# Two pairs of heads at a time: scores and value products of a causal softmax attention in double turns on one Trainium2 core

## The chip, the cores and the metric

The kernel runs on one core of a Trainium2 chip (trn2). The metric is the device time in microseconds (us) of one execution, the median of several. Five engines work from their own instruction streams and meet at semaphores: TensorE (PE; its weight loads are shown apart as PEld), VectorE (DVE), ScalarE (ACT), GpSimd (POOL) and SyncE (SP), which here only issues DMAs.

## What is computed

The input x is (32, 256, 128), float32. Six residual blocks follow each other. The first four (two small feed-forward products with tanh, a linear attention, a spectral product) work on groups of four 128-row tiles; this change leaves them alone. The last two are the causal softmax attention with 16 heads, and a spectral product on its result:

```python
q = jnp.einsum('qdh,bcd->bhcq', Q, x) * sq
k = jnp.einsum('qdh,bcd->bhcq', K, x) * sq
v = jnp.einsum('vdh,bcd->bhcv', V, x) * sv
att = jnp.einsum('bhcq,bhCq->bhcC', q, k) / d_query
att = jnp.where(causal, att, -jnp.inf)
p = jax.nn.softmax(att, axis=-1)
y = jnp.einsum('bhcC,bhCv->bhcv', p, v)
z = jnp.einsum('dvh,bhcv->bcd', W, y) * (math.sqrt(d_embed / d_value) / num_heads)
...
x = x + _L1_attn_ref(_layernorm(x, axis=-1), L1_attn_Q, L1_attn_K, L1_attn_V, L1_attn_W)
x = x + 0.5 * _L1_ffn_ref(_layernorm(x, axis=-1), L1_ffn_w_freq_real, L1_ffn_w_freq_imag, L1_ffn_bias)
```

## The kernel before, in words

Everything stays in SBUF. After the first four blocks (about 265 us) comes the softmax stage: 32 batches of 256 tokens, each worked through in 8 turns, one turn per pair of heads. Pair number n = 8b + p is pair p of batch b; j = p % 2 names the buffer. The order of the work is written out by hand in one `batch` function per engine, and each engine runs its own list; `batches` unrolls the first two and last two batches and loops over the rest, two at a time.

A pair passes through these steps:

- QK, `qk_product` (L1013 to L1015): queries and keys of the two heads, six matmuls over all 128 rows, into the one bank BANK_QK. ACT copies the bank as rounded values (`qk_high`, L739), DVE writes what the rounding left (`qk_low`, L501). Only then is the bank free for the next QK.
- S, `scores` (L1028): twelve matmuls that each use half of the rows of the array (64), the two heads side by side, into two of the four S banks.
- mask and row maximum on DVE (`mask_scores`, L515), exp with row sums on ACT (`exp_head`, L753, once per head), 1/sum on DVE (`inv_sum`, L523), the scaling on POOL (`scale_probs`, L321 and L323).
- T, `probs_transpose` (L1041): six transposes over all 128 rows, four into BANK_T and two into the bank behind it. DVE copies the four (`probs_T`, L530), ACT the two (L762).
- PV, `products` (L1058): eight matmul passes that each use half of the columns of the array, into the other half of that second bank. ACT copies y out (`y_out`, L777).

Before the change, turn n of PE is: QK of pair n+3, S of n+2, PV of n-1, one extra piece, T of n. The extra pieces, E below, are: in turn 0 the transposes XT (L1005) and ZT (L1075), in turns 1 to 3 the output projection Z of the batch before (`project_out`, L1067, in steps of 12, 12 and 8 of its 32 matmul passes, the last with the spectral product SP, L1080 and L1083), in turns 4 to 7 V, the values of the next batch (`values`, L1047 to L1049). The end of the stage (the last pairs, the last projection and spectral product) is written out behind the loops.

The steps of the loop that matter, in PE's list:

```python
pe.wait_ge(qklo_ready, count(n + 3))
qk_product(n + 3, (p + 3) % PAIRS, jb if p + 3 < PAIRS else 1 - jb, 1 - j)
```

## Time and profile before

| | |
|---|---|
| three timed runs | 1364.82, 1366.13, 1367.47 us; median 1366.13 us |
| the profiled execution | 1366.64 us, of which the span is 1364.9 us |
| busy over the span | PE 1303.4 us (95%), PEld 1081.4 (79%), DVE 1030.2 (75%), ACT 970.6 (71%), POOL 592.0 (43%) |
| mean granted clock of TensorE | 0.991 of full speed |

The profile comes from one execution; its times are from the span's start. "Busy" counts instructions that do work. A matmul's record is longer than the distance to the next one's start, since matmuls are pipelined, so PE can show as busy without a gap and still lose time between two starts; distances of starts tell more than busy shares.

### The profile page before, as it was taken

How to read it: one execution, taken by the hardware profiler on the slowest of the kernel's cores; microseconds unless marked ns; L12 is line 12 of the kernel's file. 1: busy time of each engine (PE TensorE's matmuls, PEld its weight loads, DVE VectorE, ACT ScalarE, POOL GpSimd, SP SyncE). 2: the span in 40 equal slices, each digit the busy share in tenths (PEclk: the TensorE clock that was granted, in tenths of full speed). 3: DMA queues.
4: the chain of work that ended last, by engine and by line, in shares of the span. 5: the costliest groups of instructions: out<-in, count | busy, mean ns of one | idle time of the engine just before them, and what ended most of it. 6: DMA issues, size and time to landing. Idle time of an engine off the chain costs nothing.

```text
span 1364.9 us, 38712 instructions
## 1 busy us (share of the span) xinstructions
PE 1303.4 (95%) x11331; PEld 1081.4 (79%) x11331; DVE 1030.2 (75%) x4813; ACT 970.6 (71%) x3377; POOL 592.0 (43%) x913
## 2 busy tenths in 40 slices
PE   5799977899999999999999999999999999999996
PEld 4688866778888888888888888888888888888884
DVE  6977689777777777777777777777777777777763
ACT  4754467587777777777777777777777777777772
POOL 5821158344444444444444444444444444444442
PEclk9999999999999999999999999999999999999997
DMA  8000000000000000000000000000000000000000
GB/s 206 1 1 0 1 1 1 0 2 2 2 9 0 8 0 8 0 8 0 8 0 8 0 8 0 8 0 8 0 8 0 8 0 8 0 8 0 9 2 16
DMA packets 14301, 11.79 MB, mean 9 GB/s; under 512 B 710, under 2 KB 12523, under 8 KB 14059
## 3 DMA queue, kind: packets, MB, share of 16 engines
q1 hardware_dynamic: 14240, 11.19, 3.0%
q8 instruction: 23, 0.38, 0.1%
q14 instruction: 28, 0.22, 0.1%
q10 hardware_dynamic: 10, 0.00, 0.0%
HBM read 7.00 MB, written 4.19 MB: 8 GB/s over the span
## 4 chain that ended last, share of the span: by engine, by line
PE 90%; issue 3%; DVE 3%; ACT 2%; DMA 1%; POOL 1%; SPq 1%; DVEq 0%; POOLq 0%; ACTq 0%
PE ps L1028 16%; PE ps L1058 15%; PE ps L1041 13%; PE ps L1067 10%; PE ps L1013 5%; PE ps L1014 4%; PE ps L1015 4%; PE ps L1047 4%; PE ps L1048 2%; PE ps L1049 2%; PE ps L900 2%; PE ps L922 2%; PE ps L942 2%; PE ps L960 1%; PE ps L1083 1%
## 5 line engine op out<-in xcount | busy, mean ns | idle before, releaser
L321 POOL TENSOR_TENSOR pr<-pr,rinv 128x256 f32<-128x256 f32 x256 | 158.1, 618 | 611.6 <-DVE rinv L523 611.6
L753 ACT ACTIVATE pr<-ps,neg_max 128x128 f32<-128x128 f32 (+1 forms) x1024 | 418.5, 428 | 0.0
L515 DVE CUSTOM_DVE_ANT_0 ps<-ps,mask 128x128 f32<-128x128 f32 (+1 forms) x1024 | 334.7, 386 | 0.0
L530 DVE COPY pT<-ps 128x512 f32<-128x512 f32 x256 | 177.2, 692 | 194.3 <-PE ps L1041 194.0
L323 POOL TENSOR_TENSOR pr<-pr,rinv 128x512 f32<-128x512 f32 x256 | 266.4, 1040 | 0.0
L501 DVE TENSOR_TENSOR qk_lo<-ps,qk_hi 128x512 fp32r<-128x512 f32 x256 | 176.2, 688 | 71.7 <-ACT qk_hi L739 71.7
L1058 PE MATMUL ps<-pT,space 128*64 128x256 f32 (+1 forms) x2048 | 224.3, 340 | 2.3 <-DVE pT L530 2.3
L739 ACT CAST qk_hi<-ps 128x512 fp32r<-128x512 f32 x256 | 150.4, 587 | 106.9 <-PE ps L1015 106.7
L1041 PE MATMUL ps<-ident,pr 128*128 128x128 f32 x1536 | 217.2, 274 | 4.7 <-POOL pr L323 3.3
L753 ACT ACTIVATION_READ_ACCUMULATOR pr<-ps,neg_max 128x1 f32 x1024 | 217.8, 213 | 0.0
L1041 PEld LDWEIGHTS ps<-ident,pr 128*128 128x128 f32 x1536 | 179.0, 141 | 31.2 <-issue 8.4
L762 ACT COPY pT<-ps 128x256 f32<-128x256 f32 x256 | 95.4, 373 | 145.0 <-PE ps L1041 133.2
L1058 PEld LDWEIGHTS ps<-pT,space 128*64 128x64 f32 x2048 | 124.7, 136 | 75.5 <-DVE pT L530 3.4
L1028 PE MATMUL ps<-qk_hi 64*128 64x128 f32 (+1 forms) x1024 | 169.1, 327 | 0.0
L1013 PE MATMUL ps<-x_hi,wqk_hi 128*128 128x256 f32 x512 | 166.1, 324 | 0.1
L1014 PE MATMUL ps<-x_lo,wqk_hi 128*128 128x256 f32 x512 | 143.8, 281 | 0.0
L1015 PE MATMUL ps<-x_hi,wqk_lo 128*128 128x256 f32 x512 | 143.6, 281 | 0.0
L515 DVE DVE_READ_ACCUMULATOR2_ANT neg_max<- 128x1 f32 x1024 | 142.8, 139 | 0.0
L1028 PE MATMUL ps<-qk_lo,qk_hi 64*128 64x128 f32 (+1 forms) x1024 | 142.6, 275 | 0.0
L1067 PE MATMUL ps<-wz,space 128*128 128x128 f32 x1024 | 141.9, 288 | 0.5 <-ACT z_xT L783 0.5
L1028 PE MATMUL ps<-qk_hi,qk_lo 64*128 64x128 f32 (+1 forms) x1024 | 142.2, 274 | 0.0
L1067 PEld LDWEIGHTS ps<-wz,space 128*128 128x128 f32 x1024 | 124.0, 195 | 16.8 <-issue 15.9
(165 smaller groups left out, 2374.5 us busy)
## 6 DMA issues: line engine op xcount, KB each, us to landing
out<-x_all SPq DMA_DIRECT2D x16, 256.0 KB, 2.3
x_all<-L_attn_x SPq DMA_DIRECT2D x1, 768.0 KB, 6.7
x_all<-L_attn_x SPq DMA_DIRECT2D x1, 512.0 KB, 4.6
space<-L_attn_Q SPq DMA_DIRECT2D x1, 512.0 KB, 15.6
space<-L_attn_K SPq DMA_DIRECT2D x1, 512.0 KB, 9.7
space<-L_attn_V SPq DMA_DIRECT2D x1, 512.0 KB, 11.3
space<-L_attn_W SPq DMA_DIRECT2D x1, 512.0 KB, 11.7
dft_s<-dft SPq DMA_DIRECT2D x1, 192.0 KB, 2.5
```

The source lines that it names most:

```text
L323: nc.gpsimd.tensor_tensor(pr[:, j, :, 1:3, :].rearrange("p h b k -> p h (b k)"), pr[:, j, :, 1:3, :].rearrange("p h b k -> p h (b k)"), r[ ...
L501: nc.vector.tensor_tensor(qk_lo[:, j].rearrange("p s k -> p (s k)"), ps[:, BANK_QK, :], qk_hi[:, j].rearrange("p s k -> p (s k)").bitcast( ...
L515: last = nc.vector.tensor_tensor_reduce(o, o, mask[:, T - w:T], -1.0, -MASKED, ALU.add, ALU.min, neg_max[:, j, 2 * h + qt:2 * h + qt + 1])
L530: nc.vector.tensor_copy(pT[:, j].rearrange("p h b q -> p (h b q)")[:, 0:512], ps[:, BANK_T, :]).then_inc(pTa_ready, 1)
L753: last = nc.scalar.activation(dst, ps[:, BANK_S + 2 * j + h, qt * P:qt * P + w], ACT.Exp, bias=neg_max[:, j, at:at + 1], scale=-1.0, accum ...
L1013: mm(o, wqk_hi[:, s, of_pair], x_hi[:, jb, :], start=True, stop=False, skip_group_check=True)
L1014: mm(o, wqk_hi[:, s, of_pair], x_lo[:, jb, :], start=False, stop=False, skip_group_check=True)
L1015: last = mm(o, wqk_lo[:, s, of_pair], x_hi[:, jb, :], start=False, stop=True, skip_group_check=True)
L1028: last = mm(ps[:, BANK_S + 2 * j + h, qt * P:qt * P + w], q[of_head, j, 0, qt * P:(qt + 1) * P], key[of_head, j, 1, 0:w], start=(k == 0), ...
L1041: last = tr(ps[:, BANK_T + k // 4, (k % 4) * P:(k % 4 + 1) * P], pr[:, j, k // 3, k % 3, :], ident[:])
L1058: last = mm(y_bank[k * DV:(k + 1) * DV, kt * P:T], vv[:, jb, kt, h * DV:(h + 1) * DV], pT[:, j, k, 0:2, :] if kt == 0 else pT[:, j, k, 2, ...
L1067: last = mm(ps[:, BANK_X, t * D:(t + 1) * D], yT[:, j, p, t * P:(t + 1) * P], wz[:, p, :], start=(p == 0), stop=(p == PAIRS - 1), skip_gro ...
```

## The change

Turns are paired. In each turn p, PE now does QK of pair n+2, the extra piece, and T of pair n-1. In an odd turn there follow S of n+1, S of n+2, PV of n-2 and PV of n-1, in a row. The extra pieces move by one turn: V of the next batch in turns 5 to 7 and the following 0, XT and ZT in turn 1, Z in turns 2 to 4.

`pr` gets a third buffer. The last two transposed blocks of a pair and its y share a half of bank 7 (BANK_Y) one after the other: T of an even pair writes the first half, T of an odd pair the second; PV of n-2 writes its y over the first half and PV of n-1 over the second, once the blocks have been copied out. `y_out` is called once per two turns and copies both halves as one 128x512 block (for the first pair of every second batch, where the ring of y wraps, two of 128x256).

ACT and DVE follow: an even turn of ACT begins with exp of the first head of pair n+1, then the QK copy of n+2, and ends with exp of the second head; an odd turn does both heads of the next even pair and then `y_out`. DVE masks two pairs in a row at the end of an odd turn. The diff, cut to its core (what is left out renames arguments, keeps waits in step, and adapts the steps ahead of the loops):

```diff
-        pr = sb("pr", [P, 2, 2, 3, P])
+        pr = sb("pr", [P, 3, 2, 3, P])
...
+        BANK_QK, BANK_S, BANK_X, BANK_T, BANK_Y = 0, 1, 5, 6, 7
...
-        LN_TURN, W_TURN, ADD_TURN, V_TURN, Z_TURN = 1, 1, 4, 4, 5
+        X_TURN, LN_TURN, W_TURN, V_TURN, Z_TURN = 1, 2, 2, 5, 6
+
+        def pr_of(p):
+
+            return 0 if p % 2 == 0 else 1 + p % PAIRS // 2 % 2
...
-                    if not (first and p == 0):
-                        probs_T(n - 1, 1 - j)
-                    inv_sum(n, j)
-                    if p == LN_TURN and not last:
+                    if p % 2 == 0:
+                        inv_sum(n, j)
+                    if p == 0 and above_0(b - 1):
+                        z_norm(b - 2)
+                    if p == X_TURN + 1 and not last:
                         x_low(b + 1, 1 - jb)
                     if p == LN_TURN and has_batch(b + 2):
                         ln_soft_stats(b + 2, jb)
-                    if p == LN_TURN + 2 and has_batch(b + 2):
+                    if p == LN_TURN + 3 and has_batch(b + 2):
                         ln_soft_norm(b + 2, jb)
-                    if p == ADD_TURN and not first:
+                    if p == Z_TURN and not first:
+                        z_stats(b - 1)
+                    if p % 2 == 1:
+                        inv_sum(n, j)
+                    if not (last and p >= PAIRS - 2):
+                        qk_low(n + 2, j)
+                    if p == W_TURN + 2 and not first:
                         add_z(b - 1)
                         if above_0(b - 1):
                             add_spectral(b - 2, b)
-                    if p == Z_TURN and not first:
-                        z_stats(b - 1)
-                    if p == Z_TURN + 1 and not first:
-                        z_norm(b - 1)
-                    if not (last and p >= PAIRS - 3):
-                        qk_low(n + 3, 1 - j)
-                    if not (last and p >= PAIRS - 2):
-                        mask_scores(n + 2, j)
+                    if not (first and p == 0):
+                        probs_T(n - 1, 1 - j)
+                    if p % 2 == 1 and not (last and p == PAIRS - 1):
+                        mask_scores(n + 1, 0)
+                        mask_scores(n + 2, 1)

             batches(dve, batch)
+            z_norm(B - 2)
             probs_T(B * PAIRS - 1, 1)
-            add_z(B - 1)
             add_spectral(B - 2, B)
+            add_z(B - 1, B + 1)
             z_stats(B - 1)
             z_norm(B - 1)
-            add_spectral(B - 1, B + 1)
+            add_spectral(B - 1, B + 2)
...
-            def exp_head(n, j, h):
...
                 act.wait_ge(max_ready, count(2 * n + (1 + h)))
                 if h == 0:
-                    if above_0(n - 1):
-                        act.wait_ge(pt_done, count(n - 1))
+                    kept = n - 1 if buf == 0 else n - 3
+                    if above_0(kept):
+                        act.wait_ge(pt_done, count(kept))
                     if above_0(n - 1):
                         act.wait_ge(rinv_ready, count(n - 1))
...
-                nc.scalar.copy(pT[:, j].rearrange("p h b q -> p (h b q)")[:, 512:768], ps[:, BANK_T + 1, 0:256]).then_inc(pTb_ready, 1)
+                nc.scalar.copy(pT[:, j].rearrange("p h b q -> p (h b q)")[:, 512:768], ps[:, BANK_Y, j * T:(j + 1) * T]).then_inc(pTb_ready, 1)
...
-            def y_out(b, jb, p):
-                act.wait_ge(pv_done, count(b * PAIRS + (p + 1)))
-                if p == 0:
-                    if above_0(b - 1):
-                        act.wait_ge(w_done, count(b - 1))
-                nc.scalar.copy(yT[:, jb, p, :], y_bank).then_inc(y_ready, 1)
...
+            def y_out(b, jb, p, first=False):
+
+                act.wait_ge(pv_done, count(b * PAIRS + p))
+                if p == 1 and above_0(b - 1):
+                    act.wait_ge(w_done, count(b - 1))
+                at = jb * PAIRS + p - 1
+                if at > 0:
+                    nc.scalar.copy(y_ring[:, (at - 1) * T:(at + 1) * T], ps[:, BANK_Y, :]).then_inc(y_ready, 1)
+                else:
+                    if not first:
+                        nc.scalar.copy(yT[:, 1, PAIRS - 1, :], ps[:, BANK_Y, 0:T])
+                    nc.scalar.copy(yT[:, 0, 0, :], ps[:, BANK_Y, T:2 * T]).then_inc(y_ready, 1)
...
             def batch(b, jb, first=False, last=False):
                 for p in range(PAIRS):
                     n, j = b * PAIRS + p, p % 2
-                    if not (first and p == 0):
-                        probs_T(n - 1, 1 - j)
-                    if not (last and p >= PAIRS - 3):
-                        qk_high(n + 3, 1 - j)
-                    if not (last and p >= PAIRS - 1):
-                        exp_head(n + 1, 1 - j, 0)
-                        exp_head(n + 1, 1 - j, 1)
-                    if p > 0:
-                        y_out(b, jb, p - 1)
-                    elif not first:
-                        y_out(b - 1, 1 - jb, PAIRS - 1)
-                    if p == 0 and above_0(b - 1):
+                    if p % 2 == 0:
+                        exp_head(n + 1, 1, 0, pr_of(p + 1))
+                    if not (last and p >= PAIRS - 2):
+                        qk_high(n + 2, j)
+                    if p == X_TURN and above_0(b - 1):
                         z_xT_out(b - 2)
-                    if p == 0 and not last:
+                    if p == X_TURN and not last:
                         x_high(b + 1, 1 - jb)
                     if p >= V_TURN and not last:
                         values_out(b + 1, 1 - jb, p - V_TURN)
+                    if p == 0 and not first:
+                        values_out(b, jb, 3)
+                    if not (first and p == 0):
+                        probs_T(n - 1, 1 - j)
+                    if p % 2 == 0:
+                        exp_head(n + 1, 1, 1, pr_of(p + 1))
+                    else:
+                        if not (last and p == PAIRS - 1):
+                            exp_head(n + 1, 0, 0, 0)
+                            exp_head(n + 1, 0, 1, 0)
+                        y_out(b, jb, p, first)
...
             batches(act, batch)
+            z_xT_out(B - 2)
             probs_T(B * PAIRS - 1, 1)
-            y_out(B - 1, 1, PAIRS - 1)
-            z_xT_out(B - 2)
-            z_xT_out(B - 1)
+            last_y_out()
+            z_xT_out(B - 1, B + 1)
...
-            def probs_transpose(n, j):
+            def probs_transpose(n, j, buf, y_calls):
                 pe.wait_ge(pn_ready, count(n + 1))
                 if above_0(n):
                     pe.wait_ge(pTa_ready, count(n))
                 for k in range(6):
                     if k == 4 and above_0(n):
                         pe.wait_ge(pTb_ready, count(n))
-                        pe.wait_ge(y_ready, count(n))
-                    last = tr(ps[:, BANK_T + k // 4, (k % 4) * P:(k % 4 + 1) * P], pr[:, j, k // 3, k % 3, :], ident[:])
+                        pe.wait_ge(y_ready, count(y_calls))
+                    to = ps[:, BANK_T, k * P:(k + 1) * P] if k < 4 else ps[:, BANK_Y, j * T + (k - 4) * P:j * T + (k - 3) * P]
+                    last = tr(to, pr[:, buf, k // 3, k % 3, :], ident[:])
                 last.then_inc(pt_done, 1)
...
-            def products(n, p, jb, j):
+            def products(n, p, jb, j, half):
...
                 for kt in range(BT):
                     for k in range(2):
                         h = 2 * p + k
-                        last = mm(y_bank[k * DV:(k + 1) * DV, kt * P:T], vv[:, jb, kt, h * DV:(h + 1) * DV],
+                        last = mm(ps[k * DV:(k + 1) * DV, BANK_Y, half * T + kt * P:(half + 1) * T], vv[:, jb, kt, h * DV:(h + 1) * DV],
...
                 for p in range(PAIRS):
                     n, j = b * PAIRS + p, p % 2
-                    if not (last and p >= PAIRS - 3):
-                        pe.wait_ge(qklo_ready, count(n + 3))
-                        qk_product(n + 3, (p + 3) % PAIRS, jb if p + 3 < PAIRS else 1 - jb, 1 - j)
                     if not (last and p >= PAIRS - 2):
-                        scores(n + 2, jb if p + 2 < PAIRS else 1 - jb, j)
-                    if p > 0:
-                        products(n - 1, p - 1, jb, 1 - j)
-                    elif not first:
-                        products(n - 1, PAIRS - 1, 1 - jb, 1 - j)
-
-                    if p == 0:
+                        pe.wait_ge(qklo_ready, count(n + 2))
+                        qk_product(n + 2, (p + 2) % PAIRS, jb if p + 2 < PAIRS else 1 - jb, j)
+
+                    if p == 0 and not first:
+                        pe.wait_ge(v_ready, count(4 * b + 3))
+                        values(b, jb, 3)
+                    if p == X_TURN:
                         pe.wait_ge(v_ready, count(4 * (b + 1)))
                         if not last:
                             x_transpose(b + 1, 1 - jb)
...
                     if p >= V_TURN and not last:
                         values(b + 1, 1 - jb, p - V_TURN)
-                    probs_transpose(n, j)
+
+                    if not (first and p == 0):
+                        probs_transpose(n - 1, 1 - j, pr_of(p - 1), b * (PAIRS // 2) + p // 2)
+                    if p % 2 == 1:
+                        if not (last and p == PAIRS - 1):
+                            scores(n + 1, jb if p + 1 < PAIRS else 1 - jb, 0)
+                            scores(n + 2, jb if p + 2 < PAIRS else 1 - jb, 1)
+                        pe.wait_ge(pTb_ready, count(n))
+                        if p > 1:
+                            products(n - 2, p - 2, jb, 1, 0)
+                        elif not first:
+                            products(n - 2, PAIRS - 1, 1 - jb, 1, 0)
+                        products(n - 1, p - 1, jb, 0, 1)

             batches(pe, batch)
-            products(B * PAIRS - 1, PAIRS - 1, 1, 1)
             pe.wait_ge(out_ready, B - 2)
             spectral_transpose(B - 2)
+            probs_transpose(B * PAIRS - 1, 1, pr_of(PAIRS - 1), B * PAIRS // 2)
             pe.wait_ge(z_xT_ready, B - 1)
-            project_out(B - 1, 1, (0, BT * PAIRS))
             spectral_product(B - 2)
+            products(B * PAIRS - 1, PAIRS - 1, 1, 1, 0)
             pe.wait_ge(out_ready, B - 1)
+            project_out(B - 1, 1, (0, BT * PAIRS), only=True)
             spectral_transpose(B - 1)
             pe.wait_ge(z_xT_ready, B)
             spectral_product(B - 1)
```

PE in turn 5 of a looped batch, before, from the end of S through PV to V (each instruction waits for what stands in brackets):

```order
L1028 MATMUL ps<-qk_lo,qk_hi 128x256 x2
L1028 MATMUL ps<-qk_hi,qk_lo 128x256 x2
L1058 MATMUL ps<-pT,space 64x256 [waits pTb_ready,pTa_ready]
L1058 MATMUL ps<-pT,space 64x256
L1058 MATMUL ps<-pT,space 64x128 x2
L1147 REGISTER_ALU
L1047 MATMUL ps<-v_hi,x_hi 128x512 [waits v_ready]
```

The same place of an odd turn in the changed kernel, from the end of the second S to the next QK:

```order
L1050 MATMUL ps<-qk_lo,qk_hi 128x256 x2
L1050 MATMUL ps<-qk_hi,qk_lo 128x256 x2
L1081 MATMUL ps<-pT,space 64x256 [waits pTb_ready,pTa_ready]
L1081 MATMUL ps<-pT,space 64x256
L1081 MATMUL ps<-pT,space 64x128 x2
L1081 MATMUL ps<-pT,space 64x256 [waits pTb_ready,pTa_ready]
L1081 MATMUL ps<-pT,space 64x256
L1081 MATMUL ps<-pT,space 64x128 x2
L1035 MATMUL ps<-x_hi,wqk_hi 128x256 [waits qklo_ready]
```

The second PV has moved up to the first, and QK, which stood before S, now comes straight after PV.

ACT before, one turn (the QK copy, two heads of exp, y):

```order
L738 REGISTER_ALU [waits qk_done]
L739 CAST qk_hi<-ps 128x512 [waits s_done]
L743 REGISTER_ALU
L753 ACTIVATE pr,rsum<-ps,neg_max 128x128 [waits rinv_ready,pt_done,max_ready]
L753 ACTIVATE pr,rsum<-ps,neg_max 128x256
L753 ACTIVATE pr,rsum<-ps,neg_max 128x128 [waits max_ready]
L753 ACTIVATE pr,rsum<-ps,neg_max 128x256
L777 COPY space<-ps 128x256 [waits pv_done]
```

ACT in the changed kernel, from the exp of an odd turn into the even turn behind it:

```order
L762 ACTIVATE pr,rsum<-ps,neg_max 128x128 [waits rinv_ready,pt_done,max_ready]
L762 ACTIVATE pr,rsum<-ps,neg_max 128x256
L751 REGISTER_ALU
L762 ACTIVATE pr,rsum<-ps,neg_max 128x128 [waits max_ready]
L762 ACTIVATE pr,rsum<-ps,neg_max 128x256
L788 COPY space<-ps 128x512 [waits pv_done]
L751 REGISTER_ALU
L762 ACTIVATE pr,rsum<-ps,neg_max 128x128 [waits rinv_ready,pt_done,max_ready]
L762 ACTIVATE pr,rsum<-ps,neg_max 128x256
L744 REGISTER_ALU
L747 CAST qk_hi<-ps 128x512 [waits s_done,qk_done]
```

The QK copy now stands behind three heads of exp and the y copy.

## Rows read from the trace of the kernel before

**Rows 1.** Busy time by stretch: start:end, us, PE, PEld, DVE, ACT, POOL, PEclk, DMA

```profile
400.00:1300.00 900.00, 899.53 (x8266) 745.57 (x8264) 680.93 (x3247) 683.97 (x2510) 390.11 (x532) 1.00 0.01 4
...
1333.00:1364.90 31.90, 19.59 (x122) 14.48 (x118) 9.70 (x47) 8.14 (x33) 7.26 (x11) 0.74 0.06 17
```

**Rows 2.** Timeline, one turn with V: start, us from start to end, instruction

```profile
803.56 0.81 PE L1041 MATMUL ps<-ident,pr 128*128 128x128 f32 x6
804.13 0.37 PE L1013 MATMUL ps<-x_hi,wqk_hi 128*128 128x256 f32 x1
...
804.41 0.69 DVE L530 COPY pT<-ps 128x512 f32<-128x512 f32 x1 [0.50 <-PE ps L1041]
...
804.81 0.28 PE L1015 MATMUL ps<-x_hi,wqk_lo 128*128 128x256 f32 x1
805.02 0.33 PE L1028 MATMUL ps<-qk_hi 64*128 64x128 f32 x2
...
805.41 0.34 PE L1028 MATMUL ps<-qk_hi 64*128 64x256 f32 x2
805.58 0.28 PE L1028 MATMUL ps<-qk_lo,qk_hi 64*128 64x256 f32 x2
...
805.70 0.28 PE L1028 MATMUL ps<-qk_hi,qk_lo 64*128 64x256 f32 x2
805.91 0.87 PE L1058 MATMUL ps<-pT,space 128*64 128x256 f32 x8
806.71 0.50 PE L1047 MATMUL ps<-v_hi,x_hi 128*128 128x512 f32 x1
```

**Rows 3.** Timeline of PE at the stage's start: QK into V; QK after a wait

```profile
266.34 0.28 PE L1015 MATMUL ps<-x_hi,wqk_lo 128*128 128x256 f32 x1
266.46 0.39 PE L1047 MATMUL ps<-v_hi,x_hi 128*128 128x512 f32 x1
...
268.03 0.39 PE L1013 MATMUL ps<-x_hi,wqk_hi 128*128 128x256 f32 x1
...
268.73 0.28 PE L1015 MATMUL ps<-x_hi,wqk_lo 128*128 128x256 f32 x1
```

**Rows 4.** Timeline of PE near the end: T straight into S

```profile
1333.73 1.21 PE L1041 MATMUL ps<-ident,pr 128*128 128x128 f32 x6 [0.16 <-POOL pr L323]
1334.87 0.33 PE L1028 MATMUL ps<-qk_hi 64*128 64x128 f32 x2
```

**Rows 5.** Timeline of PE: Z of 12 and of 8 passes, SP, T

```profile
1319.61 1.60 PE L1067 MATMUL ps<-wz,space 128*128 128x128 f32 x12
...
1328.80 1.16 PE L1067 MATMUL ps<-wz,space 128*128 128x128 f32 x8
...
1330.35 0.82 PE L1041 MATMUL ps<-ident,pr 128*128 128x128 f32 x6
```

**Rows 6.** Line L1005 (XT, two per batch): its count, first and last start, from 400 us

```profile
L1005 PE MATMUL ps<-ident,xn x54: 272/300/330, 406.6 to 1282.5; 128*128 128x128 f32 x54
```

**Rows 7.** The same line from 270 to 310 us: the first looped XT and the next

```profile
L1005 PE MATMUL ps<-ident,xn x4: 272/301/330, 274.8 to 306.4; 128*128 128x128 f32 x4
```

**Rows 8.** Timeline of DVE: qk_low, mask of one head

```profile
805.82 0.69 DVE L501 TENSOR_TENSOR qk_lo<-ps,qk_hi 128x512 fp32r<-128x512 f32 x1 [0.64 <-ACT qk_hi L739]
806.44 0.30 DVE L515 CUSTOM_DVE_ANT_0 ps<-ps,mask 128x128 f32<-128x128 f32 x1
...
807.03 0.14 DVE L515 DVE_READ_ACCUMULATOR2_ANT neg_max<- 128x1 f32 x1
```

**Rows 9.** Timeline of ACT: the QK copy, two heads of exp, the next copy

```profile
805.20 0.59 ACT L739 CAST qk_hi<-ps 128x512 fp32r<-128x512 f32 x1 [0.42 <-PE ps L1015]
805.68 0.37 ACT L753 ACTIVATE pr<-ps,neg_max 128x128 f32<-128x128 f32 x1
...
807.28 0.39 ACT L777 COPY space<-ps 128x256 f32<-128x256 f32 x1
```

**Rows 10.** Timeline of PE at the end: the last projection

```profile
1349.56 6.46 PE L1067 MATMUL ps<-wz,space 128*128 128x128 f32 x32 [0.46 <-ACT z_xT L783]
```

More of the change, by code:

```diff
@@ L173, in build @@
         neg_max = sb("neg_max", [P, 2, 4]); rsum = sb("rsum", [P, 2, 4]); rinv = sb("rinv", [P, 2, 4])
-        pr = sb("pr", [P, 2, 2, 3, P])
+        pr = sb("pr", [P, 3, 2, 3, P])
         pT = sb("pT", [P, 2, 2, 3, P])
         vv = space[:, 0:2 * BT * H * DV].rearrange("p (r t n) -> p r t n", r=2, t=BT)
-        yT = space[:, 2 * BT * H * DV:].rearrange("p (r a t) -> p r a t", r=2, a=PAIRS)
+        y_ring = space[:, 2 * BT * H * DV:]
+        yT = y_ring.rearrange("p (r a t) -> p r a t", r=2, a=PAIRS)
         ps = ctx.enter_context(nc.psum_tensor("ps", [P, 8, 512], F32))
@@ L224, in build @@
         V_BANKS, W_BANKS = (4, 7), (0, 6)
[L225 to L227 removed]
+        BANK_QK, BANK_S, BANK_X, BANK_T, BANK_Y = 0, 1, 5, 6, 7
+        FIRST_V_BANKS = (BANK_X, BANK_T, BANK_Y, BANK_X)
         FFN1, LIN, FFN2, SPEC1 = range(4)
@@ L315, in _, with scale_probs @@
             phases(pool, [[(5, g_inv_std(phase))] for phase in (FFN1, LIN, FFN2, SPEC1)])
-            def scale_probs(n, j):
+            def scale_probs(n, j, buf):
                 pool.wait_ge(rinv_ready, count(n + 1))
                 r = rinv[:, j, :].rearrange("p (h q) -> p h q", h=2)
-                nc.gpsimd.tensor_tensor(pr[:, j, :, 0, :], pr[:, j, :, 0, :],
+                nc.gpsimd.tensor_tensor(pr[:, buf, :, 0, :], pr[:, buf, :, 0, :],
                                         r[:, :, 0:1].to_broadcast([P, 2, P]), ALU.mult)
-                nc.gpsimd.tensor_tensor(pr[:, j, :, 1:3, :].rearrange("p h b k -> p h (b k)"),
-                                        pr[:, j, :, 1:3, :].rearrange("p h b k -> p h (b k)"),
+                nc.gpsimd.tensor_tensor(pr[:, buf, :, 1:3, :].rearrange("p h b k -> p h (b k)"),
+                                        pr[:, buf, :, 1:3, :].rearrange("p h b k -> p h (b k)"),
                                         r[:, :, 1:2].to_broadcast([P, 2, 2 * P]), ALU.mult).then_inc(pn_ready, 1)
@@ L342, in batch @@
                 for p in range(PAIRS):
-                    scale_probs(b * PAIRS + p, p % 2)
+                    scale_probs(b * PAIRS + p, p % 2, pr_of(p))
                     if p == LN_TURN and has_batch(b + 2):
@@ L531, in probs_T, with add_z @@
                                       ps[:, BANK_T, :]).then_inc(pTa_ready, 1)
-            def add_z(b):
-                dve.wait_ge(w_done, count(b + 1))
+            def add_z(b, w_after=None):
+                dve.wait_ge(w_done, count(b + 1 if w_after is None else w_after))
                 nc.vector.tensor_tensor(xb(b), ps[:, BANK_X, 0:BT * D], xb(b), ALU.add).then_inc(x_ready, 1)
@@ L588, in _ @@
             mask_scores(0, 0)
-            qk_low(2, 0)
             mask_scores(1, 1)
@@ L770, in values_out, with last_y_out, z_xT_out @@
                 nc.scalar.copy(vv[:, j, c % 2, 512 * (c // 2):512 * (c // 2) + 512], ps[:, bank, :]).then_inc(v_ready, 1)
-            def y_out(b, jb, p):
-                act.wait_ge(pv_done, count(b * PAIRS + (p + 1)))
-                if p == 0:
-                    if above_0(b - 1):
-                        act.wait_ge(w_done, count(b - 1))
-                nc.scalar.copy(yT[:, jb, p, :], y_bank).then_inc(y_ready, 1)
-            def z_xT_out(b):
+            def y_out(b, jb, p, first=False):
[9 more added lines that the diff above has]
+                    nc.scalar.copy(yT[:, 0, 0, :], ps[:, BANK_Y, T:2 * T]).then_inc(y_ready, 1)
+            def last_y_out():
+                act.wait_ge(pv_done, B * PAIRS)
+                nc.scalar.copy(yT[:, 1, PAIRS - 1, :], ps[:, BANK_Y, 0:T]).then_inc(y_ready, 1)
+            def z_xT_out(b, w_after=None):
                 act.wait_ge(z_tr_done, count(b + 1))
                 if above_0(b):
-                    act.wait_ge(w_done, count(b + 1))
+                    act.wait_ge(w_done, count(b + 1 if w_after is None else w_after))
                 nc.scalar.copy(z_xT[:], ps[:, BANK_X, T:2 * T]).then_inc(z_xT_ready, 1)
@@ L793, in _ @@
             values_out(0, 0, 2, FIRST_V_BANKS[2])
-            qk_high(2, 0)
-            exp_head(0, 0, 0)
-            exp_head(0, 0, 1)
+            exp_head(0, 0, 0, 0)
+            exp_head(0, 0, 1, 0)
             values_out(0, 0, 3, FIRST_V_BANKS[3])
@@ L1061, in products, with project_out @@
                 last.then_inc(pv_done, 1)
-            def project_out(b, j, steps):
-                pe.wait_ge(y_ready, count(PAIRS * (b + 1)))
+            def project_out(b, j, steps, only=False):
+                pe.wait_ge(y_ready, count(PAIRS // 2 * (b + 1) + 1))
                 for k in range(*steps):
@@ L1068, in project_out @@
                               start=(p == 0), stop=(p == PAIRS - 1), skip_group_check=True)
-                if not above_0(b) and steps[1] == BT * PAIRS:
+                if (only or not above_0(b)) and steps[1] == BT * PAIRS:
                     last.then_inc(w_done, 1)
```

9 lines of the change are left out of this document (2 added, 7 removed).

## The prediction

> **What bounds the kernel now.** First the busy times by stretch [rows 1]: from 400 to 1300 us PE shows 899.5 of 900 us at full granted clock, DVE and ACT about 680 each. So the softmax stage is PE's, and only PE's distances from start to start say what a turn costs. Second, the length of a batch: the 54 starts of XT from 406.6 to 1282.5 are 27 batches, 26 distances, 33.69 us each [rows 6]. Third, one turn in the timeline [rows 2]. A piece that follows one of its own mode starts before the former ends by the pipelining: QK's first matmul starts 0.24 us before the end of T. A piece in another mode (all rows, half the rows, half the columns) starts only 0.07 us before that end: QK into S (805.09 against 805.02), S into PV, PV into V. Against the usual step of 0.12 that is 0.09 us lost at each of three changes per turn. V behind PV also opens slowly, 0.50 us for its first matmul, against 0.39 behind QK, where no change lies between [rows 3]: another 0.11.
>
> **What the change takes from PE.** From the same rows, in distances from a piece's start to the next one's start. Before: T 0.57, QK 0.89, S 0.89, PV 0.80 [rows 2], two turns 6.30; extra pieces per batch 4 V of 0.80, Z 1.44 twice, Z with SP 1.55, XT with ZT 0.49, together 8.1; sum 4 x 6.30 + 8.1 = 33.3, and 0.4 of small waits makes the 33.69.
>
> Now, for two turns: QK behind PV 0.70 + 0.12 = 0.82 (opening as after a wait [rows 3]), T 0.57, QK behind T 0.68 + 0.12 = 0.80, T into S 0.74 (six transposes last 0.81 [rows 2], and S starts 0.07 before T's end, 1334.87 against 1334.94 [rows 4]), S into S 0.80, S 0.89, PV into PV 0.71, PV 0.75. For the two joints that no row shows (S into S, PV into PV) I take the step within a mode; the upper end is that they cost the full 0.09. Sum 6.08. Extra pieces behind QK lose their opening: V 0.70, Z of twelve 12 x 0.11 = 1.34 (the difference of the 12 and the 8 passes is 0.44 for four [rows 5]), Z with SP 1.45, XT with ZT 0.44. Per batch 4 x 0.70 + 2 x 1.34 + 1.45 + 0.44 = 7.37. PE alone would need 4 x 6.08 + 7.37 = 31.7 us a batch, 2.0 less than now.
>
> A rule of the Trainium skill bears on the joints. The rows: the second half of S opens with a step of 0.17 us (805.41 to 805.58), though neither rows nor mode change there. TensorE: Matmul & The Clock Gate, Part 3, says that a weight load overlaps running matmuls only when its row groups differ. By it S into S, with the same row groups, would show its load in full; the trace does not bear it out in general, since QK's six matmuls all use the same rows and still follow each other every 0.12 us. By the rule each of the eight joints of a batch would cost 0.05 us more (0.17 less 0.12), PE alone 32.1 instead of 31.7.
>
> **What it adds: a wait.** The QK bank is single, so QK of pair n+4 waits for qk_low of n+3. That now hangs on ACT, where the QK copy of n+3 stands behind both heads of exp of n+1, the y copy, and the first head of n+2; and these wait for masks of an S that comes late in the odd turn. I follow this loop from one QK of an odd turn (pair n+2) to the next (n+4), with hand-overs between engines at 0.04 us, as T's end at 804.37 against DVE's start at 804.41 [rows 2]; the other end is 0.11, ACT's start after QK's end (805.20 against 805.09 [rows 9]).
>
> - QK start to S of n+1: 0.82 + E + 0.74 = 1.56 + E, E being the odd turn's extra piece.
> - S start to the end of its last 128x256 pair: 805.98 less 805.02 = 0.96 [rows 2], hand-over 0.04.
> - mask of one head: 806.44 to 807.17, 0.73 [rows 8], hand-over 0.04.
> - exp of two heads: 805.68 to 807.28, 1.60 [rows 9]. The second head's mask is ready 0.2 us before its exp starts.
> - y copy, 128x512: as the QK copy's step, 805.20 to 805.68, 0.48 [rows 9]. PV of n-1 ends 3.24 us after the start of S, the exps 3.37 us after it: it is just not late.
> - exp of one head of n+2: 0.80.
> - QK copy 0.59, hand-over 0.03, qk_low 0.69 [rows 8, 9], hand-over 0.05.
>
> After S starts this is 6.01, so the loop takes 7.57 + E. PE's own work for two turns is 6.08 + E + E', with E' the even turn's piece. Turns 7 to 0 and 5 to 6: loop 8.27, PE 7.48, so PE waits 0.8. Turns 1 and 2: loop 8.01, PE 7.86, plus about 0.15 since Z now waits for the y copy and for x_low; I take 8.05. Turns 3 and 4: 8.91 against 8.87. A batch takes 2 x 8.27 + 8.05 + 8.91 = 33.50. Of the 2.0 us that PE gains, 1.8 become waits before QK.
>
> Beside the loop: DVE in an even turn (1/sum, then z_norm, x_low with statistics, or z_stats, all under 1.1 us) has from 3.6 to 5.2 us after S; add_z and the T copies have the time PE waits. qk_low of n+2 is done some 0.4 us before S of n+2. POOL scales a pair 2 us before its T. The third pr buffer is what lets exp of n+2 go before T of n; it costs no instruction. Four copies of y fewer per batch save ACT about 1.3 us, none of it on PE's path but what the loop counts. No DMA moves.
>
> **The sum.** 28 full batches save 0.19 us each: 5.3. The first batches gain nothing: the first takes 31.5 us from XT to XT [rows 7], and the loop gives 4 x 7.57 + 0.22 + 2 x 0.70 = 31.9; with the second, and one later first y, I add 1.3. At the end, S of the last pair to the last Z took 1349.56 - 1334.87 = 14.7 us [rows 4, 10]; the last two pairs now overlap, I count 12.0 by the durations above, and the sum x + z no longer waits for SP behind Z (0.7): 3.4 less. Together 5.3 - 1.3 + 3.4 = 7.4 us below the profiled execution's 1366.6, so 1359.2. The median of the runs lies 0.5 below that execution: 1359.
>
> **Rivals.**
> *The loop is longer than counted, slower.* Place: ACT, between the mask of n+1 and the QK copy of n+3. If the hand-overs PE to DVE, DVE to ACT and DVE to PE cost 0.11 instead of 0.04 (the QK copy's start speaks for it; T's copies against it), and the y copy waits 0.1 for PV because the two joints cost 0.09 each, the loop grows by 0.3, four times a batch: +1.2 x 28 = 34 us, 1393. It decides from 0.07 us on: that is where the 7.4 us are used up. With the hand-overs alone, 0.2, it is 1381. Chance 0.22.
> *PE stays the bound.* If QK of n+4 does not wait, because qk_low comes earlier than I read from the order (the loop under 6.7), PE needs 31.7 us a batch: 2.0 x 28 + 3.4 = 59 less, 1307. The durations on ACT and DVE are steady to 0.01 us, which speaks against it. Half of it, by a loop some 0.25 shorter: 1331. Chance of the two 0.12.
> *The joints cost as much as the changes before* (the change does not do what it says): PE alone 32.4 a batch, still under the loop but for turns 3 and 4 (+0.2): 1365. Chance 0.08.
> *The clock falls.* In the last 32 us PE is busy for 19.6 and the granted clock is 0.74 [rows 1], its lower level part of the time. With 0.8 us of waiting in 8.3, PE is still 95% busy. If a tenth of the stage ran at the lower level, matmuls at twice their time would add 0.1 x 31.7 a batch, some 90 us. Chance 0.02. TensorE: Matmul & The Clock Gate, Part 4, in the Trainium skill, says that transposes do not count as activity for the clock in the way of matmuls; this trace, with 48 of them a batch, holds the full clock from 400 to 1300 us.
>
> **How the numbers follow.** My case 0.56, at 1359, with 1350 to 1368 by 0.08 us of the loop either way; the longer loop 0.22, PE as the bound or half of that 0.12, the joints 0.08, the clock 0.02. A measurement of this kernel tells about 0.2% from no change, so faster is under 1363.4 and slower over 1368.9. Faster: 0.46 of my case, 0.12 of PE as the bound, 0.02 of the joints, together 0.60. Same: 0.10 of my case, 0.04 of the joints, 0.02 of the longer loop, 0.16. Slower: 0.20 of the longer loop, 0.02 of the joints, 0.02 of the clock, 0.24. The range of 8 in 10 leaves out the full PE-bound case and the longest loop: 1335 to 1382.
>
> **What would show it.** PE waits for DVE's qk_low about 0.8 us before the QK of turns 1 and 7, about 0.2 before turn 3 and hardly before turn 5; XT to XT takes 33.5 us; S, S, PV, PV with one change between S and PV; ACT never idle between the exp of n+1 and the QK copy of n+3. It would be wrong if PE shows no wait on qk_low, if ACT waits for PV before the y copy, or if DVE is the one that is late with the mask.

## The result: 4.3% slower, and where the profile shows it

The changed kernel takes 1426.39 us (median of 4 runs, 1421.88 to 1428.73) against 1365.74 us before: ratio 1.0434, interval 1.0411 to 1.0457. The forecast was 1359, with 1335 to 1382 as its range. The profiled execution has 1428.73 us and a span of 1427.0.

The page of the changed kernel, busy times, queues and the costliest wait:

```profile
PE 1279.1 (90%) x11323; PEld 1093.3 (77%) x11331; DVE 1032.3 (72%) x4813; ACT 945.3 (66%) x3265; POOL 591.6 (41%) x913
...
q14 instruction: 93, 0.75, 0.2%
q8 instruction: 23, 0.38, 0.1%
...
L1035 PE MATMUL ps<-x_hi,wqk_hi 128*128 128x256 f32 x512 | 173.6, 339 | 86.1 <-DVE qk_lo L505 85.9
```

PE's busy time fell by 24 us (1303.4 before; with the clock up all through, in the run with four memsets below, it is 1252.0), as an order with fewer changes of mode should make it, and 86 us of waiting for qk_low came up. The stretch from 400 to 1300 us, answering [rows 1] (same columns), and the line of XT, answering [rows 6]:

```profile
400.00:1300.00 900.00, 826.16 (x7719) 709.31 (x7715) 637.74 (x3050) 620.86 (x2262) 364.84 (x500) 0.97 0.01 4
```

```profile
L1027 PE MATMUL ps<-ident,xn x50: 270/273/421, 417.9 to 1280.7; 128*128 128x128 f32 x50
```

Fifty starts are 24 batches' distance: 862.8 / 24 = 35.95 us per batch, against 33.69 before and 33.50 forecast. But the batches are not alike. In the records they alternate for most of the stage: 37.0, 34.7, 37.0, 34.7, and the one batch that lies in the loop's first pass, ahead of the first jump back, takes 33.73. Something happens once per pass of the loop, which holds two batches. That pass takes 71.87 us against 67.39 before (mean of the 13 distances between the ends of DVE's passes).

What it is shows where DVE jumps back. Timeline of DVE there: start, us, instruction, idle time before it and what ended it:

```profile
843.16 0.46 DVE L519 CUSTOM_DVE_ANT_0 ps<-ps,mask 128x256 f32<-128x256 f32 x1
843.53 0.13 DVE L519 DVE_READ_ACCUMULATOR2_ANT neg_max<- 128x1 f32 x1
845.19 0.18 DVE L527 RECIPROCAL rinv<-rsum 128x4 f32<-128x4 f32 x1 [1.52 <-ACT pr L762]
847.71 0.60 DVE L563 TENSOR_SCALAR z_xn<-x_all,z_mv,z_rstd 128x128 f32 x2 [2.34 <-issue]
848.23 0.68 DVE L505 TENSOR_TENSOR qk_lo<-ps,qk_hi 128x512 fp32r<-128x512 f32 x1
```

PE in the same place:

```profile
844.58 0.81 PE L1064 MATMUL ps<-ident,pr 128*128 128x128 f32 x6
848.96 0.58 PE L1035 MATMUL ps<-x_hi,wqk_hi 128*128 128x256 f32 x1 [3.57 <-DVE qk_lo L505]
849.34 0.42 PE L1036 MATMUL ps<-x_lo,wqk_hi 128*128 128x256 f32 x1
```

The stretch behind the wait, and the next one (columns as in [rows 1]):

```profile
848.80:852.20 3.40, 3.24 (x15) 3.24 (x16) 1.48 (x4) 1.23 (x3) 1.61 (x2) 0.51 0.00 0
852.20:870.00 17.80, 17.63 (x173) 15.38 (x173) 13.15 (x62) 11.67 (x45) 6.21 (x9) 1.00 0.00 0
```

And the DMA queues from 840 to 850 us:

```profile
q14 instruction: 3, 0.02, 0.9%
```

Read together: DVE stands for 2.34 us with nothing to wait for ("issue"), three packets of instructions of 8192 bytes come in at 843.2, 845.6 and 848.2, PE waits 3.57 us, and for the next 3.4 us it has its lower clock (0.51, 1.2 GHz), so its matmuls there have steps of 0.21 us in place of 0.12. Before, no instruction packet comes between 398 and 1281.9 us; now there are five per pass. The clock fell once in each of the 12 passes between 400 and 1240 us, behind waits of PE of 3.4 to 3.7 us.

### The profile page after: what moved, and what is told of

Same layout as the page of the kernel before. It is cut to its first block, busy times and chain, and to the rows that moved or that the text cites. A ratio compares the mean times of both kernels' runs of the same rounds, so it can differ in the third digit from the quotient of the medians.

```text
span 1427.0 us, 38829 instructions
## 1 busy us (share of the span) xinstructions
PE 1279.1 (90%) x11323; PEld 1093.3 (77%) x11331; DVE 1032.3 (72%) x4813; ACT 945.3 (66%) x3265; POOL 591.6 (41%) x913
## 4 chain that ended last, share of the span: by engine, by line
PE 41%; issue 20%; DVE 20%; ACT 15%; DMA 1%; POOL 1%; DVEq 1%; SPq 1%; ACTq 0%; POOLq 0%
ACT pr L762 11%; PE ps L1090 7%; PE ps L1064 6%; DVE neg_max L519 4%; DVE pT L534 4%; PE ps L1035 4%; DVE qk_lo L505 4%; DVE ps L519 3%; ACT qk_hi L747 3%; PE ps L1050 3%; PE ps L1037 2%; PE ps L1036 2%; PE ps L922 2%; PE ps L1081 2%; PE ps L944 2%
## 5 line engine op out<-in xcount | busy, mean ns | idle before, releaser
L762 ACT ACTIVATE pr<-ps,neg_max 128x128 f32<-128x128 f32 (+1 forms) x1024 | 429.5, 438 | 166.9 <-DVE neg_max L519 166.9
L519 DVE CUSTOM_DVE_ANT_0 ps<-ps,mask 128x128 f32<-128x128 f32 (+1 forms) x1024 | 329.3, 389 | 21.3 <-issue 20.1
L1035 PE MATMUL ps<-x_hi,wqk_hi 128*128 128x256 f32 x512 | 173.6, 339 | 86.1 <-DVE qk_lo L505 85.9
L762 ACT ACTIVATION_READ_ACCUMULATOR pr<-ps,neg_max 128x1 f32 x1024 | 225.6, 220 | 0.0
L1064 PEld LDWEIGHTS ps<-ident,pr 128*128 128x128 f32 x1536 | 187.8, 145 | 20.1 <-issue 1.9
L1035 PEld LDWEIGHTS ps<-x_hi,wqk_hi 128*128 128x128 f32 x512 | 99.0, 193 | 129.4 <-DVE qk_lo L505 107.3
L1081 PE MATMUL ps<-pT,space 128*64 128x256 f32 (+1 forms) x2048 | 197.2, 335 | 0.7 <-ACT pT L771 0.5
L747 ACT CAST qk_hi<-ps 128x512 fp32r<-128x512 f32 x256 | 154.9, 605 | 61.8 <-PE ps L1037 61.8
L1050 PE MATMUL ps<-qk_hi 64*128 64x128 f32 (+1 forms) x1024 | 157.3, 304 | 0.0
L1090 PE MATMUL ps<-wz,space 128*128 128x128 f32 x1024 | 132.5, 278 | 4.9 <-DVE x_lo L499 2.3
```

The lines of the kernel that those rows point to most:

```text
L519: last = nc.vector.tensor_tensor_reduce(o, o, mask[:, T - w:T], -1.0, -MASKED, ALU.add, ALU.min, neg_max[:, j, 2 * h + qt:2 * h + qt + 1])
L747: nc.scalar.copy(qk_hi[:, j].rearrange("p s k -> p (s k)"), ps[:, BANK_QK, :]).then_inc(qkhi_ready, 1)
L762: last = nc.scalar.activation(dst, ps[:, BANK_S + 2 * j + h, qt * P:qt * P + w], ACT.Exp, bias=neg_max[:, j, at:at + 1], scale=-1.0, accum ...
L1035: mm(o, wqk_hi[:, s, of_pair], x_hi[:, jb, :], start=True, stop=False, skip_group_check=True)
L1050: last = mm(ps[:, BANK_S + 2 * j + h, qt * P:qt * P + w], q[of_head, j, 0, qt * P:(qt + 1) * P], key[of_head, j, 1, 0:w], start=(k == 0), ...
L1064: last = tr(to, pr[:, buf, k // 3, k % 3, :], ident[:])
```

## The theories

**A, code loading.** DVE's loop is 367 instructions. If its memory takes code in blocks of 8192 bytes and holds a few, it may matter where in a block the loop starts. The change leaves four fewer DVE instructions ahead of the loop, and one more in it. In the records of a pass, DVE has four instructions between the first stop and the second (the loop's own register step, that of the next wait, the 1/sum, one more): as if the loop's first four stood at the end of one block and the next block were late as well. **B, the loop of waits** itself is longer at the joint of two batches. **C, the clock** falls by itself under the new order, and DVE is only drawn along.

## Experiments: where the code stands

**Four memsets.** DVE fills four columns that nobody reads, ahead of its soft part, so the loop's code stands where it stood before.

```
+        fill = sb("fill", [P, 4])
...
+            for i in range(4):
+                nc.vector.memset(fill[:, i:i + 1], 0.0)
             ln_soft_stats(0, 0)
```

> The changed kernel with four more memsets of a column of their own on DVE ahead of its soft part, so that DVE's loop code starts at the position it has in the kernel before. Theory A (code loading: DVE's loop of 367 instructions no longer stands in its instruction memory because its first instructions lie in the last slots of a block of 128, so each of the 13 jumps back waits for two blocks and the clock falls after it): the 5 instruction packets per loop iteration are gone from the records, an iteration takes 67.3 to 67.6 us where the changed kernel takes 71.7, the granted clock stays at 1.00 in the loop, and the time is 1365 to 1372 us. Theory B (the fetches are there but hidden; the loop of waits QK, S, mask, exp is simply longer at the joint of turns 7 and 0): no change, 1426 us. Theory C (the clock falls by itself, from the idle time of the new row): still some half-clock stretches, 1410 to 1426 us.

Measured: 1369.06 us, ratio to before 1.0014 (1.0004 to 1.0023). Four memsets of 59 ns take 57 us off. The queues list 27 packets on q14 for the whole run in place of 93, with none in the loop; a pass takes 67.52 us. Page, and the stretch from 400 to 1300 us:

```profile
q14 instruction: 27, 0.22, 0.1%
```

```profile
400.00:1300.00 900.00, 855.78 (x8226) 732.82 (x8226) 692.58 (x3235) 661.36 (x2413) 390.45 (x534) 1.00 0.01 4
```

DVE at the same jump (the seventh):

```profile
812.86 0.18 DVE L528 RECIPROCAL rinv<-rsum 128x4 f32<-128x4 f32 x1
813.20 1.61 DVE L564 TENSOR_SCALAR z_xn<-x_all,z_mv,z_rstd 128x128 f32 x2 [0.17 <-issue]
```

B and C fall: the work and its order are those of the changed kernel, and the clock is 1.00.

**Two memsets, sixteen, twenty-eight, sixty-four** (the same edit with another number); the first three ran once each.

> Two memsets instead of four, one look. By theory A the loop of the changed kernel starts one to four places ahead of a block's border; four memsets carry it over. With two: either no packets in the loop and 1369 us (it stood one or two places ahead), or two misses per jump as in the changed kernel, 1426 us (three or four places). Nothing between the two.

> Sixteen memsets, one look. By theory A DVE's 367 instructions of the loop then begin at place 12 to 15 of a block and end within the third block (12 to 15 plus 367 is at most 382 of 384): no packet in the loop, 1369 us. If instead only the exact start of a block were good, packets would be back.

> Twenty-eight memsets, one look. The loop then begins at place 24 to 27 and its last 7 to 10 instructions reach into a fourth block: five packets per iteration and one late block at the jump, 1385 to 1410 us. If the memory held four blocks of the loop whatever is fetched ahead: none, 1369 us.

> As the run with four memsets, but sixty-four, so that the loop begins in the middle of a block. Theory A: the loop still touches four blocks and the one behind them, so about 5 packets per iteration stay, but only the first block is late at the jump (the second comes in while the first half block runs): one stall of 2 to 3 us instead of two, iteration 68 to 70 us, time 1375 to 1405 us. Theory B and C: 1426 us, whatever the number of memsets.

Then the kernel **before** with sixty-four, and with 124, which is four short of 128:

> The kernel before with sixty-four memsets on DVE ahead of its soft part. Theory A: it has no instruction packet in its loop only because of where its loop starts; now packets appear at each jump back (about 5 per iteration) and the time rises by up to 13 x 2.5 us, 1370 to 1400 us. If the packets were a consequence of the change's own code (one instruction more in the loop, or another engine's), none appear and the time stays at 1366 to 1368 us.

> The kernel before with 124 memsets on DVE ahead of its soft part, which puts DVE's loop code four places ahead of a multiple of 128 from where it was, that is at the place within a block that it has in the changed kernel. If the place alone decides, five packets per iteration appear with three in a row at the jump, as in the changed kernel. Theory S (the kernel before has slack on DVE that swallows the wait, PE's turns there being paced by PE): an iteration grows from 67.4 by 1 to 3 us only, the clock falls seldom, and the time is 1378 to 1410 us. Rival (the whole loss belongs to the place of the code, whatever the order of the work): it grows by 4.2 us as in the changed kernel, 1420 to 1426 us.

Measured: the mean pass (13 distances), the packets of q14 from 420 to 1240 us, the time at the lower clock from 400 to 1240 us, and where in a block of 128 the loop then starts if before's start is called 0. Each ratio, here and below, is taken against runs of the kernel before that were made beside it (medians from 1365.0 to 1367.4 us), not against the first row:

```
kernel          start  packets  pass us  low clock us  median us   ratio to before
before              0        0    67.39          0.0     1365.74
before + 64        64       60    67.97          0.0     1373.27   1.0049 (1.0031 to 1.0066)
before + 124       -4       56    71.19         41.0     1416.81   1.0355 (1.0330 to 1.0380)
changed            -4       56    71.87         47.8     1426.39   1.0434 (1.0411 to 1.0457)
changed + 2        -2       55    73.67         78.5     1452.26   one run
changed + 4         0        0    67.52          0.0     1369.06   1.0014 (1.0004 to 1.0023)
changed + 16       12        0    67.53          0.0     1370.15   one run
changed + 28       24       56    71.51         44.4     1422.09   one run
changed + 64       60       57    69.95         23.9     1406.31   1.0294 (1.0275 to 1.0312)
```

The pattern of packets is as A says. Starts at 0 and 12 bring none: the loop ends within the third block (12 + 367 = 379 of 384). At 24 its end reaches the fourth (391) and the packets are there, as at 60 and 64. So a loop of three blocks stays resident, and one that touches four is fetched anew in every pass. That five packets come and not four I read as the block behind the loop, fetched ahead. The period of 128 shows in the kernel before: 124 more instructions do what four fewer do.

The step at the block's border can be seen by eye. With two memsets the second stop comes two instructions sooner, ahead of the 1/sum and no longer behind it: two instructions of the loop stand before it at start -2, four at -4, so the border is at 0 itself. DVE at the jump:

```profile
855.03 0.18 DVE L528 RECIPROCAL rinv<-rsum 128x4 f32<-128x4 f32 x1 [3.67 <-ACT pr L765]
855.37 1.61 DVE L564 TENSOR_SCALAR z_xn<-x_all,z_mv,z_rstd 128x128 f32 x2 [0.16 <-issue]
```

The 1/sum comes 5.2 us behind the branch here and 1.5 behind it with four memsets, so the "ACT" named behind 3.67 is only the last semaphore of that wait, not what held it. The same goes for the 1.52 in the changed kernel's timeline above: it is the first stop.

The times were foretold less well than the packets. At -2, 26 us more than at -4, where I expected 1426: the clock is low for 78.5 us in place of 47.8, by falls of which many last two or three times as long. At 24, 1422 where I expected at most 1410: the fourth block is entered a few instructions ahead of the jump, so that a packet starts 0.34 us behind the branch and the next only at 1.08; I read the first as the one for the block beyond the loop, ahead of the one that the jump needs. At 60, 1406 against an end of 1405. And the kernel before at -4 ends 7 us above what I gave it. It swallows little of two stops but most of one: at start 64 its DVE stands 22.1 us in 12 passes, 1.8 each, and a pass grows by 0.58 only.

```profile
DVE pT L531 <- issue: 22.1, 12, 2.0
```

(Waits of DVE, before + 64, 420 to 1240 us: total, times, longest.) The changed kernel at 60 loses 2.4 per pass for one such stop.

**A delay in place of the packets.** Is it DVE's standing still that costs, or something else about the packets? Here no packet comes in the loop, and DVE fills 3 x 1100 elements once per pass.

```
+                    if isinstance(b, Count) and jb == 0 and p == 0:
+                        for i in range(3):
+                            nc.vector.memset(slow[:, i, :], 0.0)
                     if p % 2 == 0:
                         inv_sum(n, j)
```

> The changed kernel with four memsets (no packets in the loop), and a delay made by hand: in the first batch of each iteration DVE fills 3 x 1100 elements, some 3.5 us, ahead of the first 1/sum of turn 0, which is about what DVE stands still at the jump in the changed kernel. If DVE's standing still there is the whole loss, and the fall of the clock its consequence: an iteration takes 71 to 72 us again, half-clock stretches of 3.4 us come back behind the waits, and the time is 1415 to 1432 us, with no packet in the loop. If the packets cost by something else (their traffic, the other engines' code): 1369 to 1385 us.

> The kernel before with the same three fills ahead of DVE's first copy of turn 0 in the first batch of each iteration, no packets in its loop. If the wait is what costs: as the kernel before at the bad place, 70 to 72 us per iteration, 1405 to 1425 us. If before swallows a DVE delay and lost by the packets themselves: 1366 to 1375 us.

The fills of the first:

```profile
L604 DVE MEMSET slow<- x42: 975/975/975, 340.3 to 1269.1; 128x1100 f32 x42
```

So the delay was 2.9 us, less than I had aimed at. Changed + 4 with it: 1421.28 us, ratio 1.0417 (1.0399 to 1.0436), a pass 71.21, clock low for 37.5 us. Before with it: 1402.42 us, ratio 1.0276 (1.0254 to 1.0297), 3 us under the expected 1405. With no packet in the loop, 52 of the 57 us are back in the changed kernel, and 37 of some 50 in the kernel before: DVE's standing still is the cause, and the falls of the clock come back with it. The last run also prices the fall, since its passes alternate: 70.7 us with 3.4 us at the lower clock, 69.27 without. One fall costs 1.4 us there, a delay of 2.9 us the other 1.9. (In the changed kernel with the delay, the two passes without a fall took 69.8 us and most others 71.4: 1.6.) PE's wait behind the delay is the same in all passes of that last run, but only every second one is followed by a fall; what picks the pass no run here shows. Its waits from 400 to 1240 us, and one of the low stretches:

```profile
PE ps L1062 <- DVE pT L531: 20.1, 12, 1.7
```

```profile
834.30:837.70 3.40, 3.13 (x16) 2.91 (x16) 1.90 (x10) 1.22 (x4) 0.91 (x3) 0.51 0.00 0
```

## Experiments: the loop of waits that the forecast was built on

With the code in place the changed kernel runs at 33.76 us a batch, and PE waits for qk_low as forecast. The forecast named ACT, where the QK copy stands behind the exp of a head. In even turns it can go ahead of it:

```
-                    if p % 2 == 0:
-                        exp_head(n + 1, 1, 0, pr_of(p + 1))
                     if not (last and p >= PAIRS - 2):
                         qk_high(n + 2, j)
+                    if p % 2 == 0:
+                        exp_head(n + 1, 1, 0, pr_of(p + 1))
```

> The changed kernel with the four memsets and one thing more: in even turns ACT copies QK's high part before the exp of the second pair's first head instead of behind it. In the changed kernel's trace this copy starts 0.6 us after its matmuls are done, because the exp stands ahead of it. Theory L (the loop over the copy of QK, qk_low and the next QK sets the rate of the unrolled part, as the prediction had it, 33.5 to 33.7 us per batch): PE's wait of some 0.57 us between T and QK goes in the turns behind a row of scores, PE becomes the bound at 31.7 to 32.3 us per batch, and the time is 1310 to 1335 us. Rival (the exp so delayed makes the scale and T late instead, or another link takes its place): 1355 to 1372 us, as the run with four memsets alone.

Measured: 1337.12 us, ratio 0.9772 (0.9757 to 0.9788). A pass takes 65.60 us, 32.8 a batch, and PE's wait for qk_low from 700 to 963 us is down to four waits of 3.8 us together:

```profile
PE ps L1038 <- DVE qk_lo L506: 3.8, 4, 1.0
```

It is 2 us above my range. The four waits left are at the jumps, where z_norm stands ahead of qk_low on DVE. The next version moves it behind:

```
-                    if p == 0 and above_0(b - 1):
-                        z_norm(b - 2)
...
                         qk_low(n + 2, j)
+                    if p == 0 and above_0(b - 1):
+                        z_norm(b - 2)
```

> The version with the earlier QK copy and four memsets, and z_norm moved behind qk_low in turn 0 on DVE. There PE waited 1.0 us before the QK of turn 0 in every second batch (the batch behind the jump back) and 0.3 us in the other, with z_norm ahead of qk_low on DVE. If z_norm is what is late: these waits go, an iteration takes 64.5 to 65.0 us instead of 65.6, 1324 to 1332 us. If the wait is that of the exps before it: no change, 1335 to 1338 us.

Measured: 1326.97 us, ratio **0.9708 (0.9694 to 0.9722)**, the fastest version here, 39 us under the kernel before. A pass takes 65.11 us (0.1 over what I expected). XT and the stretch of the stage:

```profile
L1030 PE MATMUL ps<-ident,xn x54: 272/272/273, 402.3 to 1248.8; 128*128 128x128 f32 x54
```

```profile
400.00:1300.00 900.00, 889.01 (x8538) 761.36 (x8538) 694.77 (x3347) 677.54 (x2501) 402.24 (x549) 1.00 0.01 4
```

Last, the earlier copy without the memsets:

> The earlier QK copy alone, without the memsets, so with the packets at each jump. If the loss at the jump is a fixed 4.2 us per iteration: 1337 + 55 = 1392 us. If the slack won by the earlier copy (some 0.8 us per pair of turns on DVE's way) takes in a part of it: 1365 to 1385 us.

Measured: 1380.77 us, ratio 1.0088 (1.0057 to 1.0119), a pass 69.36 us. The packets are there (59), and cost 44 us in place of 57. About a quarter of the loss is gone, which I put down to the slack, and the order that is 2.3% faster than before in the one place is 0.9% slower than before in the other.

## Why the prediction was wrong, point by point

**The step that failed** is in the part on what the change adds: "No DMA moves", and beside the loop only waits of engines were listed. Instructions are fetched by DMA too. The change shortens DVE's code ahead of the loop by four, and no term stood for it. Of the 60.6 us between the medians, 57.3 go with the four memsets (1426.39 less 1369.06); the change itself is worth 1 to 2 us for the worse, against the 1367.43 of the runs made beside it (ratio 1.0014). In the trace of before the hint was an absence: not one instruction packet from 398 to 1281.9 us. The Trainium skill's page Runtime: NRT & Kernel Launch, Instruction fetch mechanics, says that a taken branch to code that is no longer held forces a fetch before execution goes on. By that rule a loop longer than what is held is paid at each jump, and the runs agree in kind, with stops of 1.5 to 2.3 us. They do not agree in the sizes that the section gives, blocks of 16 KiB and two of them: as I read it, with the next block fetched while the current one runs, a loop of 366 instructions would have been fetched in the kernel before as well. Here the packets have 8192 bytes, and three blocks stay.

**The rival "the clock falls"** had the right sign and a chance of 0.02, as a cause of its own. It is a consequence: of a loss of some 4.4 us per pass, about 1.4 to 1.6 are the lower clock behind PE's wait of 3 to 4 us, by the passes with and without a fall. The 95% busy that the forecast set against it holds for a batch; in the turns with 0.8 us of waiting in 8.3 it would be 90%.

**The loop of waits was right, to 0.1 us.** From S to S over two turns, in one of the two batches of each steady pass of the changed kernel with four memsets:

```
turns            forecast   measured
5 to 6, 7 to 0       8.27       8.30
1 to 2               8.05       8.04
3 to 4               8.91       8.99
```

PE waits for qk_low twice a batch, as forecast. The idle time is 0.74 us each (39.8 / 54). Counted from start to start, as the forecast's 0.8 is, it is 0.98, since T's record goes on for 0.24 us behind the point where the next piece would start. Its waits from 400 to 1300 us in that kernel:

```profile
PE ps L1038 <- DVE qk_lo L506: 39.8, 54, 0.9
PE ps L1093 <- DVE x_lo L500: 2.3, 13, 0.2
```

The other batch of the pass has 8.23 and 9.06 in place of 8.04 and 8.99, so a batch is 33.76 on average, not 33.50: 0.26 x 28 = 7.3 us, the largest of the terms mis-sized.

**What PE needs was right within 2%, on the safe side.** Measured steps: QK 0.82, T into S 0.75, S to PV 1.57 (I had 0.80 + 0.89), PV to QK 1.45 (0.71 + 0.75), QK behind T 0.80, T 0.57: 5.96 for two turns against 6.08. S into S costs nothing:

```profile
718.78 0.28 PE L1050 MATMUL ps<-qk_hi,qk_lo 64*128 64x256 f32 x2
718.90 0.22 PE L1050 MATMUL ps<-qk_hi 64*128 64x128 f32 x2
718.96 0.28 PE L1050 MATMUL ps<-qk_lo,qk_hi 64*128 64x128 f32 x2
```

The step over the joint is 0.12 us, the ordinary one, not the 0.17 that the prediction weighed. So the rule of the Trainium skill (TensorE: Matmul & The Clock Gate, Part 3) on weight loads of the same row groups does not show at this joint. The joint tests it weakly, since the two heads use different halves of the rows in turn there as everywhere in S; QK's six matmuls on all 128 rows, one every 0.12 us, speak against it more. Z took 1.34 where it came straight behind QK, as forecast, and 1.44 behind its wait for x_low. At 31.3 us of work a batch, the fastest version's 32.56 still hold some 1.3 us of small waits.

**Start and end.** With four memsets the way from the stage's first XT to the fifth took 117.1 us against 111.8 before: 5.3 more where I had 1.3. The clock fell for 3.4 us at 275.9, in that stretch, which is worth some 1.4 of it; the rest was not tried. The end gained 5.4 us (from the last XT to the end of the span, 77.2 against 82.6) where I had 3.4. With the batches between (911.4 against 909.6 us) and 0.8 less ahead of the stage, that is the 1.0 us between the two spans.

**The sign:** with the code in place the forecast's 1359 stands against 1369, a change worth nothing, though the mechanism was the one described. The 2.0 us a batch that PE gained all went into waits for qk_low (2 x 0.98), where the forecast had 1.8 of them; the last 0.2 of gain did not come.

## What to carry to other kernels

Count where an engine's loop code starts before judging an edit to a looped kernel (seen here for DVE alone): a handful of instructions more or fewer ahead of a loop moved this one by 4%, so look at the packets of the instruction queue and the "issue" waits at the jump first, and compare versions at the same place in the block. When a new order gains on the bounding engine and the gain turns into one wait, the cure can be in the order of the engine that the wait hangs on: here two steps swapped on ACT and one moved on DVE gave what the change alone did not.

## What the runs showed of the chip that I had not expected

- DVE's code comes in packets of 8192 bytes, 128 instructions. Loops of 366 and 367 instructions (370 and 371 with the fills) stay resident where they touch three such blocks (starts 0 and 12) and are fetched again in each pass, five packets, where they touch four (starts -4, -2, 24, 60, 64).
- A block that is late at a jump holds DVE: the loop's first instruction comes 2.8 to 3.5 us behind the branch where it otherwise comes 0.3 behind. The following block, if the loop starts just ahead of its border, costs 2.1 us more. Where the loop starts in the middle of a block only the first stop is seen.
- A wait of 3.6 us on PE was followed by 3.4 us at 1.2 GHz. A delay of 2.9 us on DVE, made by hand, brought such a stretch in every second pass of the kernel before (behind a PE wait of 1.7 us that came in every pass; the stretch cost 1.4 us) and in nearly every pass of the changed one (behind 3.2 us; it cost 1.6).
- The kernel before let one stop of 1.8 us through as 0.58 us per pass, and two stops as 3.8. The changed kernel let one through as 2.4. Busy shares did not tell them apart: DVE has 75% of the span before and 77% in the changed kernel with four memsets.
